# A two-layer decoder in one kernel: earlier expert loads, shorter waits and halves in the expert stages, one flag read moved, fewer semaphore clears

## The reference, cut to what matters

```
layer 0: x = norm(x + distance attention(x))       16 heads
         x = norm(x + gelu(x ctx^T) ctx)           6404 hidden units
         x = norm(x + experts(x))                  8 experts, 512 hidden units, relu, gates from a softmax, top 1
layer 1: x = norm(x + rotary attention(x))         16 heads
         x = norm(x + cross attention(x, ctx))     16 heads, masked, 6404 keys
         x = norm(x + block(x))                    its own norms, attention of 16 heads, 8 experts with gelu, top 1
```

```
h = act(x @ W1[e] + b1[e]);  y = h @ W2[e] (+ b2[e]);  out = sum over e of gate[:, e] * y
```

## Time and profile before

| what | value |
|---|---|
| median of 3 runs | 2414.19 us (2405.54, 2414.19, 2414.41) |
| the profiled execution's own time | 2408.9 us |
| its span, first to last instruction | 2407.2 us |
| PE busy | 2234.7 us, 93% |
| ACT busy | 1630.8 us, 68% |
| DVE busy | 954.3 us, 40% |
| POOL busy | 477.2 us, 20% |
| granted TensorE clock, mean | 0.961 of full speed |
| longest group | L1918, the exponentials of cross attention, x536, 741.5 us |

### The profile page before, as it was taken

How to read it: one execution, slowest core, us unless ns; L and a number is a source line. 1 busy time by engine, 2 the same in 40 slices (tenths; PEclk the granted TensorE clock), 3 DMA queues, 4 the chain that set the end, 5 groups by cost and what they waited for, 6 DMA issues and landing times. The chain is left out here.

```text
span 2407.2 us, 30492 instructions
## 1 busy us (share of the span) xinstructions
PE 2234.7 (93%) x12206; PEld 772.8 (32%) x12206; DVE 954.3 (40%) x1489; ACT 1630.8 (68%) x1295; POOL 477.2 (20%) x254
## 2 busy tenths in 40 slices
PE   7899999899979988999899999999999977999898
PEld 3333333344446632222211111111111122222466
DVE  6767776235441156666211111110111116886111
ACT  4899989633332223555599999999999964666433
POOL 0577776200100033666300000000000000000000
PEclk8999999999989988999999999999999996999899
DMA  1000000135643002000100010010000000000010
GB/s 44 5 9 5 5 1 1 36 137 207 214 164 149 24 0 71 1 1 1 30 16 1 1 42 1 1 42 1 1 1 1 1 6 5 1 1 1 22 35 25
DMA packets 29134, 79.03 MB, mean 33 GB/s; under 512 B 3473, under 2 KB 18977, under 8 KB 26929
## 3 DMA queue, kind: packets, MB, share of 16 engines
q1 hardware_dynamic: 15032, 30.75, 4.2%
q0 software_dynamic: 4384, 29.56, 3.5%
q10 hardware_dynamic: 9592, 16.96, 1.9%
HBM read 71.71 MB, written 5.59 MB: 32 GB/s over the span
## 5 line engine op out<-in xcount | busy, mean ns | idle before, releaser
L1918 ACT ACTIVATE crat_E<-banks 128x1536 f32<-128x1536 f32 x536 | 741.5, 1461 | 22.0 <-PE banks L1809 6.6
L1834 PE MATMUL banks<-crat_E,crat_vst 128*32 128x512 f32 (+1 forms) x3264 | 436.3, 607 | 0.5 <-ACT crat_E L1918 0.4
L1809 PE MATMUL banks<-crat_Q,mid_arena 52*128 52x512 bf16 x1600 | 322.4, 385 | 19.6 <-ACT crat_E L1918 15.3
L1945 DVE COPY crat_vst<-all_crossV 128x96 f32<-128x96 f32 x136 | 34.3, 253 | 635.3 <-PE banks L1834 635.2
L579 POOL TENSOR_TENSOR dist_wsum<-dist_wsum,dist_D 128x1024 f32<-128x1024 f32 x88 | 209.2, 2377 | 7.8
L1538 ACT ACTIVATE rotat_E<-banks 128x1024 f32<-128x1024 f32 x128 | 124.0, 1021 | 116.0 <-PE banks L1422 111.2
L434 DVE TENSOR_SCALAR dist_D<-banks,dist_k 128x512 f32<-128x512 f32 x256 | 178.6, 747 | 57.8 <-PE banks L245 57.8
L1809 PEld LDWEIGHTS banks<-crat_Q,mid_arena 52*128 52x128 bf16 x1600 | 59.3, 93 | 435.3 <-ACT crat_E L1918 301.0
L1604 DVE TENSOR_REDUCE rotat_mx<-banks 128x1 f32<-128x512 f32 x256 | 163.4, 686 | 69.9 <-PE banks L1393 68.7
L1538 ACT ACTIVATE lastat_E<-banks 128x1024 f32<-128x1024 f32 x128 | 123.9, 1020 | 85.6 <-PE banks L1414 85.6
L1604 DVE TENSOR_REDUCE lastat_mx<-banks 128x1 f32<-128x512 f32 x256 | 163.3, 686 | 36.9 <-PE banks L1393 35.1
(11 more groups left out here) (271 smaller groups left out, 2813.5 us busy)
## 6 DMA issues: line engine op xcount, KB each, us to landing
mlp_M<-in_mask POOLq DMA_DIRECT2D x28, 800.5 KB
mid_arena<-cross_k SPq DMA_DIRECT2D x42, 204.0 KB
moe_W<-in_experts SPq DMA_DIRECT2D x16, 512.0 KB, 3.6
mid_arena<-in_rot_tables ACTq DMA_DIRECT2D x8, 1024.0 KB, 19.6
mlp_C<-in_ctx SPq DMA_DIRECT2D x17, 384.0 KB, 4.6
cross_k<-mlp_kp ACTq DMA_DIRECT2D x17, 288.0 KB, 2.3
mlp_row<-in_mask POOLq DMA_DIRECT2D x1, 3202.0 KB, 12.7
mlp_M<-in_mask POOLq DMA_DIRECT2D x1, 3202.0 KB
```

Source lines behind the costliest of these rows:

```text
L1809: last = pe.matmul(PS[:, 3 * (at % 2) + k, :], K[s:s + ROWS, 2 * (g % 2) + pair, c * P:(c + 1) * P], Q[s:s + ROWS, 2 * g + pair, qh * HALF ...
L1834: last = pe.matmul(PS[32 * j:32 * j + 32, 6 + ps % 2, :], vst[keys, (ps * STEPS + c // 3) % 3, c % 3, j, :], E[keys, at // 3 % NE, at % 3, ...
L1918: act.activation(flat(E[:, at % NE, :, :]), flat(PS[:, 3 * (at % 2):3 * (at % 2) + 3, :]), ACT.Exp, scale=CROSS_SCALE).then_inc(s_e, 1)
```

## The change

1. `Names` keeps the semaphores of closed scopes in one list and clears them only when more than 100 have gathered, and at the very end.
2. `ExpertTiles` holds the expert weights, `small` and their three semaphores outside the stage. SP issues the first three loads in the norm ahead (`ln2`, `lastn2`). In `moe0` the weights lie in the tile `wide` and `small` in `wo`, both of which the rotary stage uses later.
3. `back(e, 0)` waits for combine(e-2), the last reader of its own two banks, and no longer for combine(e-1).
4. The tail: the last combine starts when half of the last back chunk is done, each of its eight instructions releases one transposed product of `acc`, the transposes of the gates stand ahead of the last back chunk, and the bias products ahead of those of `acc`. The result lies in banks 2 and 3.
5. Cross attention: each engine reads the flag inside `cross_main`; `cross_general` branches on the register. The reciprocal of the last pass is made on ACT as exp(-ln). ACT is told at the start of the stage to load the table that holds both functions.

```diff
@@ Names
     def clear(self):
-        if self.sems:
+
+        Names.used = Names.used + self.sems
+        if self.last or len(Names.used) > self.HELD:
             with self.nc.Block() as block:
                 @block.gpsimd
                 def _(pool):
-                    self.nc.clear_and_free_semaphores(self.sems)
+                    self.nc.clear_and_free_semaphores(Names.used)
+            Names.used = []
...
+class ExpertTiles:
...
+    def early(self, sp):
+        sp.dma_start(self.small, self.of_small).then_inc(self.s_small, 16)
+        for e in range(2):
+            sp.dma_start(self.W[:, e, :], self.of_experts[e]).then_inc(self.s_w[e], 16)
...
@@ routed_mlp, sync
-                sp.dma_start(small[:, 0:320], w["small"]).then_inc(s_small, 16)
-                for e in range(2):
-                    sp.dma_start(W[:, e, :], w["experts"][e]).then_inc(s_w[e], 16)
                 with sp.Fori(1, EXPERTS // 2) as i:
...
@@ routed_mlp, tensor
-                        pe.wait_ge(s_comb, e * NT + NT)
+                        pe.wait_ge(s_comb, max(e, 1) * NT if isinstance(e, int) else e * NT)
                     for t in range(NT):
...
+                        if final and t == NT // 2 - 1:
+                            last.then_inc(s_fin, 1)
                     last.then_inc(s_y, 1)
...
-                back(EXPERTS - 1, 1, FC - 1)
                 if weighted:
+                    pe.wait_ge(s_a, EXPERTS * FC + 1)
                     for t in range(NT):
-                        last = pe.transpose(PS[0:EXPERTS, 2 + t // 4, (t % 4) * P:(t % 4 + 1) * P], G[:, t, :], ident[:, :])
+                        last = pe.transpose(PS[0:EXPERTS, t // 4, (t % 4) * P:(t % 4 + 1) * P], G[:, t, :], ident[:, :])
                     last.then_inc(s_gt, 1)
-
-                pe.wait_ge(s_comb, EXPERTS * NT + NT)
-                for t in range(NT):
-                    last = pe.matmul(PS[:, t // 4, (t % 4) * P:(t % 4 + 1) * P], acc[:, t, :], ident[:, :],
-                                     start=(t % 4 == 0), stop=not weighted, skip_group_check=True)
+                back(EXPERTS - 1, 1, FC - 1, final=True)
+                pe.wait_ge(s_a, EXPERTS * FC + 2)
                 if weighted:
                     pe.wait_ge(s_gtc, 1)
                     for h in range(2):
-                        pe.matmul(PS[:, h, :], b2, half(GT, h), start=False, stop=True, skip_group_check=True)
+                        pe.matmul(PS[:, 2 + h, :], b2, half(GT, h), start=True, stop=False, skip_group_check=True)
+                for t in range(NT):
+                    pe.wait_ge(s_comb, EXPERTS * NT + t + 1)
+                    pe.matmul(PS[:, 2 + t // 4, (t % 4) * P:(t % 4 + 1) * P], acc[:, t, :], ident[:, :],
+                              start=(t % 4 == 0 and not weighted), stop=True, skip_group_check=True)
@@ routed_mlp, vector
-                def combine(e, k):
-                    dve.wait_ge(s_y, e * FC + FC + 2)
+                def combine(e, k, final=False):
+                    if final:
+                        dve.wait_ge(s_fin, 1)
+                    else:
+                        dve.wait_ge(s_y, e * FC + FC + 2)
...
+                        if final and t == NT // 2:
+                            dve.wait_ge(s_y, e * FC + FC + 2)
...
@@ cross_main, tensor
                     if g == GROUPS - 1:
+                        read["pe"] = flag_of(pe, flag)
                         pe.wait_ge(s_on, PASSES)
@@ cross_main, scalar
+                nc.scalar.preload_act_table_set("natural_log_exp_and_others")
...
+                act.wait_ge(s_xc, consumed(0))
+                read["act"] = flag_of(act, flag)
+                act.wait_ge(s_xp, len(X) + 1)
+                act.wait_ge(s_on, PASSES - 1)
+                act.activation(rec[:, :], PS[:, 0, :], ACT.Ln).then_inc(s_rl, 1)
+                act.wait_ge(s_rl, 1)
+                act.activation(rec[:, :], rec[:, :], ACT.Exp, scale=-1.0).then_inc(s_rl, 1)
@@ cross_main, vector
+                dve.wait_ge(s_xc, consumed(0))
+                read["dve"] = flag_of(dve, flag)
                 out_of(PASSES - 1)
-                dve.wait_ge(s_xp, len(X) + 1)
-                quotient(PASSES - 1, 0)
+                dve.wait_ge(s_rl, 2)
+                dve.tensor_tensor(half(On[:, GROUPS - 1, :], 1), O[:, (PASSES - 1) % 2, :], rec[:, :], ALU.mult).then_inc(s_on, 1)
...
@@ decoder (last_block alike, with tiles of its own)
-        layer_norm(nc, PS, "ln2", center, onesd, x, x, Y=6)
...
+            experts = ExpertTiles(m, wide[:, 0:2, :], wo[:, 0:320], a["small0"], a["experts0"])
+            layer_norm(nc, PS, "ln2", center, onesd, x, x, Y=6, early=experts)
```

More of the change, by code:

```diff
@@ L1709, with cross_main @@
     KEYS = 16 * 2 * len(CROSS_BLOCKS)
-def cross_main(nc, PS, name, x, cross, tiles, On, qf, flag):
+def cross_main(nc, PS, name, x, cross, tiles, On, qf, flag, read):
     PASSES = 2 * GROUPS
@@ L2064, in _ @@
             def _(sp):
-              with when(sp, flag, 0):
+              with sp.If(read["sp"] == 0):
                 sp.wait_ge(s_set, 4)
@@ L2088, in _ @@
             def _(pe):
-              with when(pe, flag, 0):
+              with pe.If(read["pe"] == 0):
                 pe.sem_inc(s_pv, 2)
@@ L2141, in _ @@
             def _(act):
-              with when(act, flag, 0):
+              with act.If(read["act"] == 0):
                 act.sem_inc(s_e, 2)
@@ L2161, in _ @@
             def _(dve):
-              with when(dve, flag, 0):
+              with dve.If(read["dve"] == 0):
                 dve.sem_inc(s_add, 2)
@@ L2290, in decoder @@
                 pre = RotaryTiles(nc, inner, a, Arena(arena), V[:, NT - 2:NT, :])
-                routed_mlp(nc, PS, "moe0", x, ident, {"small": a["small0"], "experts": a["experts0"]}, ACT.Relu, True, early=pre)
-                layer_norm(nc, PS, "ln3", center, onesd, x, x, Y=0)
+                routed_mlp(nc, PS, "moe0", x, ident, experts, ACT.Relu, True, early=pre)
+                layer_norm(nc, PS, "ln3", center, onesd, x, x, Y=2)
                 operands = RotaryOperands(nc, inner, PS, x, pre, wide, K, Qb, Kb, V, wo, tiles)
```

53 lines of the change are left out of this document (33 added, 20 removed).

## The result

| | before | after |
|---|---|---|
| median of 4 runs, us | 2414.23 | 2372.27 |
| lowest and highest | 2405.54, 2414.41 | 2366.45, 2372.42 |
| profiled execution: own time, span | 2408.9, 2407.2 | 2372.35, 2370.7 |
| PE busy in it | 93% | 94% |

The ratio is 0.9839, with a 95% interval from 0.9821 to 0.9858. The forecast was 2373 us. The ratio is not the quotient of the two medians (0.9826): by the ratio the gain is some 39 us, by the medians 42. In 32 later runs the kernel before had a median of 2408.13 us. By the spans of the two profiled executions 36.5 us went. The times of one kernel lie up to 13 us apart from run to run (2401.45 to 2414.63 in those 32), so the parts are read from the profiles, and not from the medians.

A forecast was written before the change was run, and what follows sets the result against it. It took ACT to bound the cross attention's stream, PE the expert stages, and no engine the gaps between stages. Terms 14.1 + 6.8 + 4.3 + 5.3 + 2.7 + 4 = 37.2 us off 2408.9 gave 2371.7, raised to 2373; range 2361 to 2388.

The forecast's parts named there:

- wait per bank: Expert stages, 14 changes of experts: hidden products' distance falls from 4.50 to 3.50 us, saving 14.1 us.
- clears: Between stages: 21 clear blocks become 3, so 18 barriers go, saving 6.8 us.
- starts, PE's first weight load: Begin of `moe0` and `moe1`: PE no longer waits for the load of `small`; 2.2 and 2.1, sum 4.3 us.
- tails: Ends of the expert stages: DVE starts after half a chunk; saves 1.6 us in `moe0`, 3.7 in `moe1`.
- quotient: End of cross attention: Ln and Exp replace the 3.36 us reciprocal, saving 1.7 us.
- flag: End of cross attention: reading the flag earlier hides its load behind the barrier, saving 1.0 us.
- clock, in stages that the change touches: `ln3`, `ln6` and both expert-stage starts: PE's waits go, granted clock partly holds; a third of 12, 4 us.
- rival of combine and back products in each other's way: Expert stages: running together, they stretch back(e, 0) by 0.5 to 1 us, giving back 7 to 14; 2383 us, chance 0.13.
- ACT's table loads, named as late next: Start of `moe0`: ACT issues eight table loads until 6.55 us after the begin; claimed early enough at PE's old pace.
- rival on the slow side: Cross attention's stream loses pace: 0.1 us more on each of 536 exponentials gives 2427 us; chance 0.02.
- rival with the clock held at all four places: `ln3`, `ln6` and both expert-stage starts: clock gain of 12 us in place of 4, giving 2365 us; chance 0.15.

The follow-up runs named there:

- b_early: Kernel before with only the expert stages' first loads issued in the norm ahead; median 2397.60 us, ratio 0.9963.
- b_clears: Kernel before with only the semaphore clears put together, 21 clear blocks becoming 3; median 2398.08 us, ratio 0.9961.
- b_cross: Kernel before with only the cross attention's changes (quotient by Ln and Exp, flag read inside the main block); median 2404.45 us, ratio 0.9989.

## Why the prediction was right, and where its steps were not

| term | predicted | measured |
|---|---|---|
| wait per bank | 14.1 | 14.1 |
| clears | 6.8 | 6.8 |
| starts, PE's first weight load | 4.3 | 4.4 |
| tails | 5.3 | 5.5 (1.2 of it clock) |
| quotient | 1.7 | 1.6 |
| flag | 1.0 | 0.85 |
| clock, in stages that the change touches | 4 | 9.2 |
| standstill in `ln5` | - | -1.8 |
| `dist` and other untouched stages | - | -4.0 |
| sum | 37.2 | 36.5 |

The measured column is the difference of the two profiled executions, stage by stage; its clock term is 3.8 at the starts of the expert stages and 2.4 + 1.5 + 1.5 in `ln3`, `ln6` and `lastn2`. Its parts add up to 36.6, the last 0.1 being rounding.

**Wait per bank.** Right to the tenth, alone and in the whole. The idle time behind a releaser name told the gain, because what is late next, PE's own pace, stood in the rows beside it. The rival of combine and back products in each other's way is out: the back products' x16 take 1.95 us beside a running combine.

**Clears.** Right in size. What the step left out is that code and load latencies run beside the blocks it takes away: at `moe0` alone it would have lost 0.9 us to a load, and `ln5` became 1.8 us longer with a standstill at a code fetch. I had read PE's 3.8 us as one event, and behind this first fetch there is a second one.

**Starts and tails.** Right for the starts and for `moe0`'s tail. ACT's table loads, named as late next, did make PE wait at the first back product; freeing ACT showed that little was to be had there. `moe1`'s 3.7 was read from a row of 3.22 us that was partly the low clock; the earlier trace rows have 2.05 for the same sixteen products. The edit alone gave 2.65 there and 1.6 in `moe0`, 4.3 in all against 5.3; the rest was clock.

**Cross attention.** Right, and the stream is untouched (the rival on the slow side had no hold). That rival's own sum is put wrongly: 0.1 us on each of 536 exponentials is 54 us on top of 2373, which makes the 2427 that it names, and not 2389 + 38.

**Clock.** Here the right total came from a wrong reason, and that is luck. I tied the low stretches in `ln3` and `ln6` to PE's waits in the tails. `b_early` has that wait with the clock at 1.00, and `b_clears` and `b_cross` have the old tails and norms of 6.95. The term was mis-sized as well: 9.2 us came in the stages that it spoke of (and in `lastn2`, of which it did not), not 4. The rival with the clock held at all four places had 12 and was nearer there. It was partly undone by 4.1 us that an untouched stage lost to the same cause, and by the standstill, so that 36.5 stands beside 37.2. The gain is tied to an edit by eight profiles against six at two places: at `moe0`'s start to the early loads, and in `lastn2`, 1.5 us, to the clears. The gains of `ln3` and `ln6` show up with each part of the change alone: by the spans the five parts add up to 51.6 us, and the whole gave 36.5. These two norms, counted in each part, make up 14 of the 15 us between.

What stays open: why the low stretches in `ln3` and `ln6` come and go, whether the clears' blocks or the place of the code kept the standstill out of `ln5`, and why the first stage took 461 us in some profiles and 469 in others. A kernel with longer filler products ahead of the expert stages was not tried.

## What to carry to other kernels

Where a wait is released by another engine's row and the pace without that wait stands in rows beside it, the gain can be read off to a tenth of a microsecond: look for waits that ask for more than the bank or buffer needs. Barriers and clears between stages are not only cost, they run beside loads and code fetches: ask what they hide, and start those loads earlier in the same change. Before a difference of the clock is put down to an edit, profile the unchanged kernel again and look at kernels with other edits; a right total can be two wrong parts.

## What the runs showed of the hardware

- A compare and branch on PE that skips a long block took 3.4 to 3.8 us, and in the changed kernel 1.45 us more behind it, at a place that moved with the code: two instruction packets of 16 KB, PE going on 1.4 to 1.6 us after each had landed. With the low clock that it leaves behind, 7.8 us in all.
- One norm (`lastn2`) had 3.4 us of low clock in six of six profiles with two clear blocks right ahead of it (1.0 to 1.6 us), and none, being 1.5 us shorter, in eight of eight without them. `ln4`, behind three such blocks, had none either.
- Range clears on POOL beside a norm's work held nothing up: 0.39 us of clear blocks left of 3.64.
- The granted clock's low stretches came to 135 to 186 us of an execution, and one stage with the same code took 461.0 to 469.8 us with 20.5 to 37.5 us of them. The time of one kernel goes with them: in 32 runs the kernel before took 2401.45 to 2402.05 us at a mean granted clock of 0.964 to 0.965, and 2413.43 to 2414.63 at 0.959.
